# Routing table: one-hots stored with the 16 columns innermost, a written-out count constant, and the dense rows' column left out of the products

## What is computed

```python
y = conv(x, taps)                       # 16 taps along the sequence, per channel
logits = y @ Wr                         # 4096 tokens x 8 experts
w, sel = top_k(logits, 2); w = softmax(w)
gate = sum_k w[k] * one_hot(sel[k], 8)
out = sum_e gate[e] * (y @ We[e] + be[e])
x = x + out
```

## Time and profile before

| | |
|---|---|
| median of three executions | 845.53 us (844.99 to 846.36) |
| the profiled execution | 845.81 us, of which the span of the trace is 844.1 us |
| PE busy | 740.7 us (88%) |
| DVE busy | 564.4 us (67%) |
| ACT busy | 396.8 us (47%) |
| POOL busy | 477.3 us (57%) |
| routing, from the last logits product to the first gather | 537.9 to 577.7 us of the span |

### The profile page before, as it was taken

One profiled execution on the slowest core, in us unless ns is written; L12 is line 12 of the kernel. 1 busy time (PEld: TensorE's weight loads), 2 busy tenths in 40 slices (PEclk: granted clock), 3 DMA queues, 4 the chain that ended last, 5 costly groups with the idle time before them and its releaser, 6 DMA issues.

```text
span 844.1 us, 12610 instructions
## 1 busy us (share of the span) xinstructions
PE 740.7 (88%) x3913; PEld 432.6 (51%) x3945; DVE 564.4 (67%) x831; ACT 396.8 (47%) x635; POOL 477.3 (57%) x738
## 2 busy tenths in 40 slices
PE   1745599999999999999989999657999999899994
PEld 0112244444444444444446653345788888778773
DVE  2469999999999999997734424397834654444442
ACT  2056466666768877776412524034322333333332
POOL 1037889888888888884200000003567766876864
PEclk9987899999999999999999999768999999999998
DMA  9984148899999985555698999986468778877876
GB/s 359 388 328 134 31 88 149 137 182 180 178 180 189 183 157 132 117 116 92 138 232 148 113 116 258 116 197 215 77 126 165 143 136 160 152 146 143 167 143 105
DMA packets 230270, 137.50 MB, mean 163 GB/s; under 512 B 162798, under 2 KB 195054, under 8 KB 229054
## 3 DMA queue, kind: packets, MB, share of 16 engines
q1 hardware_dynamic: 210094, 99.94, 59.0%
q0 software_dynamic: 15456, 36.47, 23.2%
q10 hardware_dynamic: 4656, 0.30, 0.5%
HBM read 80.27 MB, written 35.42 MB: 137 GB/s over the span
## 4 chain that ended last, share of the span: by engine, by line
PE 45%; DMA 13%; POOL 11%; DVE 11%; issue 9%; SPq 6%; ACT 4%; POOLq 0%; DVEq 0%; ACTq 0%
DMA out_x<-YS,IDS 8%; PE PS L1480 8%; PE PS L1452 7%; PE PS L1572 7%; PE PS L1429 7%; PE PS L1441 7%; PE PS L1507 4%; POOL out_x L751 3%; SPq L381 2%; POOL ZR L742 2%; DVE Ih L1085 2%; PE PS L1529 1%; DMA QyT<-Qy 1%; ACT Qh L818 1%; DMA QT<-Qh 1%
## 5 line engine op out<-in xcount | busy, mean ns | idle before, releaser
L1572 PE MATMUL PS<-W,ZH 128*128 x552 | 179.5, 406 | 8.2 <-DVE ZL L1339 6.1
L742 POOL DMA_INDIRECT ZR<-z_scratch,IDG x69 | 69.6, 1008 | 156.1 <-DVE IDS L1303 135.4
L1429 PE MATMUL PS<-W,QyT 128*128 128x512 bf16 x502 | 123.0, 387 | 26.8 <-DMA QyT<-Qy 15.2
L751 POOL DMA_INDIRECT out_x<-YS,IDS x69 | 110.8, 1606 | 59.1 <-SPq L560 29.7
L939 ACT ACTIVATE YS<-YS,SG 128x512 f32<-128x512 f32 x69 | 50.0, 724 | 159.9 <-DVE YS L1357 159.9
L1441 PE MATMUL PS<-W,QyT 128*128 128x512 bf16 x504 | 120.9, 381 | 0.4
L1452 PE MATMUL PS<-W,QT 128*128 128x512 bf16 x498 | 116.4, 383 | 4.4 <-DMA QT<-Qh 2.9
L1572 PEld LDWEIGHTS PS<-W,ZH 128*128 128x128 f32 x552 | 100.4, 191 | 29.7 <-issue 11.5
L1572 PE MATMUL PS<-W,ZL 128*128 x276 | 109.6, 397 | 0.0
L1339 DVE TENSOR_TENSOR ZL<-PS,ZH 128x512 fp32r<-128x512 f32 x69 | 47.7, 691 | 78.2 <-ACT ZH L928 78.2
L1429 PEld LDWEIGHTS PS<-W,QyT 128*128 128x128 bf16 x512 | 49.7, 99 | 90.0 <-DMA QyT<-Qy 17.3
(11 more groups left out here) (217 smaller groups left out, 1059.8 us busy)
## 6 DMA issues: line engine op xcount, KB each, us to landing
XW<-out_x SPq DMA_DIRECT2D x64, 240.0 KB, 4.5
X<-in_x SPq DMA_DIRECT2D x32, 256.0 KB, 10.0
out_x<-X SPq DMA_DIRECT2D x32, 256.0 KB, 3.6
z_scratch<-ZZ SPq DMA_DIRECT2D x8, 1024.0 KB, 24.1
WRAW<-in_We SPq DMA_DIRECT2D x8, 1024.0 KB, 12.6
XR<-in_x SPq DMA_DIRECT2D x20, 256.0 KB, 4.1
stage<-in_w1T SPq DMA_DIRECT2D x4, 1024.0 KB, 8.0
stage<-in_w2T SPq DMA_DIRECT2D x4, 1024.0 KB, 11.9
```

Source lines behind the costliest of these rows:

```text
L742: pool.indirect_dma_start(ZR[m % UZ][:], None, z_d, bass.IndirectOffsetOnAxis(IDG[:, m:m + 1].bitcast(U32), 0)) \
L751: pool.indirect_dma_start(x1_d, bass.IndirectOffsetOnAxis(IDS[:, m:m + 1].bitcast(U32), 0), YS[m % UN][:], None, compute_op=ALU.add).then_ ...
L1429: i = nc.tensor.matmul(GP[:, a, :], QyT[t][:, k, :], W12[:, k, o:o + CH], start=(k == 0), stop=(k == KD - 1))
L1572: x = nc.tensor.matmul(bank[i], zz[i % 2][:, k, :], W2[:, bass.ds(q, 1), part, k, :].rearrange("p o d -> p (o d)"), start=(k == 0 and n == ...
```

## The change

- AOH, BOX and BOH are stored with the 16 columns c innermost: AOH [128, 128, 16], BOX [128, 69, 16], BOH [128, 2, 69, 16]. ScalarE's copies and both operands of TensorE's products now take every 16th element, a step of 32 bytes.
- The constant that the compares read is written out: ION [128, 128, 16], where row m holds 16 times the number m. ScalarE makes it by one copy of 2048 elements from IOSB, after the logits (`lg_done`) because its place was ZZ's. The compares read ION and a row of 16 numbers (`columns`), repeated over m, in place of `over` and `along`.
- VectorE waits for that copy together with the exponentials: `route_e` 2 in place of 1.
- The dense rows' column is left out of the products: laps 0 and 2 have 15 copies and 15 products (`listed`), so that POS needs no marking there: the memset of L1265 is dropped.
- The float copy MTF (L1267) is dropped; SLB is computed from MTI.

```diff
--- before.py
+++ after.py
@@ -190,7 +190,8 @@
         WRAW = [place(f"WRAW{e}", (2 * where(e) + 1) * NEXP, [P, KD, D]) for e in range(E)]
         a = a_T + RING * D
         assert a == 2 * E * NEXP and CC * P <= UN * D and a + UZ * ZW <= a_h
-        AOH = [place(f"AOH{i}", a + CC * P // 2 * i, [P, CC, P], BF16) for i in range(2)]
+        AOH = [place(f"AOH{i}", a + CC * P // 2 * i, [P, P, CC], BF16) for i in range(2)]
+        ION = place("ION", a_h, [P, P, CC], BF16)
         ZR = [place(f"ZR{i}", a + ZW * i, [P, ZW]) for i in range(UZ)]
         YS = [place(f"YS{i}", a_h + D * i, [P, D]) for i in range(UN)]
         ZH = [place(f"ZH{i}", a_h + D * (UN + i), [P, KD, P], F32R) for i in range(2)]
@@ -202,7 +203,7 @@
         PM = place("PM", a + D, [P, OH])
         SEL = place("SEL", a + D + OB, [P, OH * E])
         LGS = [place(f"LGS{g}", a + 2 * D + NCB * g, [P, NCB]) for g in range(NQ)]
-        BOH = [place(f"BOH{i}", a + CC * MT * i, [P, CC, 2, MT], BF16) for i in range(2)]
+        BOH = [place(f"BOH{i}", a + CC * MT * i, [P, 2, MT, CC], BF16) for i in range(2)]
         a += CC * MT * 2
         ZDH, ZDL = (place(n, a + D * i, [P, KD, P], F32R) for i, n in enumerate(("ZDH", "ZDL")))
         a += 2 * D
@@ -237,7 +238,7 @@
         CNT = place("CNT", a, [P, E, NT], BF16)
         TRI, ONB, IOSB = (place(n, a + NR // 2 + P // 2 * i, [P, P], BF16) for i, n in enumerate(("TRI", "ONB", "IOSB")))
         CUM = place("CUM", a_s + 8 * D + NR, [P, E, NT], BF16)
-        BOX = [place(f"BOX{i}", a_T + RING * D + CC * P + CC * MT // 2 * i, [P, CC, MT], BF16) for i in range(2)]
+        BOX = [place(f"BOX{i}", a_T + RING * D + CC * P + CC * MT // 2 * i, [P, MT, CC], BF16) for i in range(2)]
         assert 2 * CC * P // 2 + CC * MT <= UZ * ZW
         a += NR // 2 + 3 * P // 2
         IOS = place("IOS", a, [P, P], I32)
@@ -253,7 +254,7 @@
         a += 8 * E + 8 * UN
         GTS = place("GTS", a, [P, NT, 2])
         a += NT * 2
-        POS, MTF = (place(n, a + NK * i, [P, NK]) for i, n in enumerate(("POS", "MTF")))
+        POS = place("POS", a, [P, NK])
         MTI = place("MTI", a + 2 * NK, [P, NK], I32)
         SLB, MTB = (place(n, a + 3 * NK + NK // 2 * i, [P, NK], BF16) for i, n in enumerate(("SLB", "MTB")))
         a += 4 * NK
@@ -364,13 +365,13 @@
 
             return TORD.index((w, c)) + 1
 
-        def along(t, q, n):
-
-            return t[:, CC * q:CC * q + CC].rearrange("p (c o) -> p c o", o=1).broadcast_to([P, CC, n])
-
-        def over(t, first, n):
-
-            return t[:, first:first + n].rearrange("p (o n) -> p o n", o=1).broadcast_to([P, CC, n])
+        def columns(t, q, n):
+
+            return t[:, CC * q:CC * q + CC].rearrange("p (o c) -> p o c", o=1).broadcast_to([P, n, CC])
+
+        def listed(q):
+
+            return CC if q % 2 else ND
 
 
 
@@ -899,6 +900,9 @@
                 act.wait_ge(x1_out[b], 16 * B)
             act.wait_ge(z_out[0], 16 * NQ)
             nc.scalar.dma_start(ZD[:], bass.AP(z_d.tensor, ND * ZW, [[OB * ZW, P], [SEG, NQ], [1, NI]])).then_inc(zd_in, 16)
+            act.wait_ge(lg_done, 1)
+            act.wait_ge(route_v, 4)
+            nc.scalar.copy(ION[:], IOSB[:].rearrange("p (m o) -> p m o", o=1).broadcast_to([P, P, CC])).then_inc(route_e, 1)
             act.wait_ge(route_v, VM2)
             nc.scalar.activation(EX[:], M2[:], ACT.Exp).then_inc(route_e, 1)
             act.wait_ge(zdt_done, 1)
@@ -913,8 +917,8 @@
                 act.wait_ge(boh_done, 2 * q + 1)
                 if q >= 2:
                     act.wait_ge(tab_done, q - 1)
-                for c in range(CC):
-                    i = nc.scalar.activation(BOH[q % 2][:, c, 0, :], BOX[q % 2][:, c, :], ACT.Copy, scale=float(c + 1 + CC * (q // 2)))
+                for c in range(listed(q)):
+                    i = nc.scalar.activation(BOH[q % 2][:, 0, :, c], BOX[q % 2][:, :, c], ACT.Copy, scale=float(c + 1 + CC * (q // 2)))
                 i.then_inc(num_done, 1)
 
             high(E // 2)
@@ -1241,7 +1245,7 @@
             dve.wait_ge(cnt_done, 1)
             nc.vector.tensor_tensor_scan(CUM[:].rearrange("p e n -> p (e n)"), MROW[:].rearrange("p e n -> p (e n)"),
                                          CNT[:].rearrange("p e n -> p (e n)"), 0.0, ALU.mult, ALU.add).then_inc(cnt_done, 1)
-            dve.wait_ge(route_e, 1)
+            dve.wait_ge(route_e, 2)
             v(nc.vector.tensor_scalar(P1[:], EX[:], 1.0, None, ALU.add))
             v(nc.vector.reciprocal(P1[:], P1[:]))
             v(nc.vector.tensor_tensor(P2[:], P1[:], EX[:], ALU.mult))
@@ -1262,11 +1266,9 @@
                 v(nc.vector.tensor_tensor(CAND[:], oh[:], upto[:], ALU.mult))
                 v(nc.vector.tensor_reduce(POS[:, NT * k:NT * k + NT], CAND[:], AX.X, ALU.add))
 
-            v(nc.vector.memset(POS[:].rearrange("p (k n) -> p k n", k=2)[:, :, ND], -float(P * P)))
             v(nc.vector.tensor_scalar(MTI[:], POS[:], 1.0 / P, 0.5 / P - 0.5, ALU.mult, ALU.add))
-            v(nc.vector.tensor_copy(MTF[:], MTI[:]))
             nc.vector.tensor_copy(MTB[:], MTI[:])
-            v(nc.vector.scalar_tensor_tensor(out=SLB[:], in0=MTF[:], scalar=-float(P), in1=POS[:], op0=ALU.mult, op1=ALU.add))
+            v(nc.vector.scalar_tensor_tensor(out=SLB[:], in0=MTI[:], scalar=-float(P), in1=POS[:], op0=ALU.mult, op1=ALU.add))
 
             dve.wait_ge(zdh_done, 1)
             nc.vector.tensor_tensor(ZDL[:].rearrange("p k m -> p (k m)"), bank[6],
@@ -1277,10 +1279,10 @@
                     dve.wait_ge(tab_done, q - 1)
                     dve.wait_ge(num_done, q - 1)
 
-                nc.vector.tensor_tensor(BOX[h][:], over(IOSB, 0, MT), along(MTB, q, MT), ALU.is_equal).then_inc(boh_done, 1)
+                nc.vector.tensor_tensor(BOX[h][:], ION[:, 0:MT, :], columns(MTB, q, MT), ALU.is_equal).then_inc(boh_done, 1)
                 dve.wait_ge(boh_done, 2 * q + 1)
-                nc.vector.tensor_scalar(BOH[h][:, :, 1, :], BOX[h][:], PIDX[h], None, ALU.mult).then_inc(boh_done, 1)
-                nc.vector.tensor_tensor(AOH[h][:], over(IOSB, 0, P), along(SLB, q, P), ALU.is_equal).then_inc(oh_done, 1)
+                nc.vector.tensor_scalar(BOH[h][:, 1, :, :], BOX[h][:], PIDX[h], None, ALU.mult).then_inc(boh_done, 1)
+                nc.vector.tensor_tensor(AOH[h][:], ION[:], columns(SLB, q, P), ALU.is_equal).then_inc(oh_done, 1)
 
             v(nc.vector.tensor_tensor(GE[:], IOSF[0:1, 0:MT].rearrange("p (m o) -> p m o", o=1).broadcast_to([1, MT, E]),
                                       END[0:1, :].rearrange("p (o e) -> p o e", o=1).broadcast_to([1, MT, E]), ALU.is_ge))
@@ -1542,8 +1544,8 @@
             for q in range(NK // CC):
                 pe.wait_ge(oh_done, q + 1)
                 pe.wait_ge(num_done, q + 1)
-                for c in range(CC):
-                    i = nc.tensor.matmul(bank[7][:, 0:2 * MT], AOH[q % 2][:, c, :], BOH[q % 2][:, c, :, :].rearrange("p v m -> p (v m)"),
+                for c in range(listed(q)):
+                    i = nc.tensor.matmul(bank[7][:, 0:2 * MT], AOH[q % 2][:, :, c], BOH[q % 2][:, :, :, c].rearrange("p v m -> p (v m)"),
                                          start=(q == 0 and c == 0), stop=(q == NK // CC - 1 and c == CC - 1))
                 i.then_inc(tab_done, 1)
                 dense(q)
```

## The result

The changed kernel takes 854.42 us (median of four, 853.78 to 856.70) against 845.26 us for the kernel before: 1.0108 times as long, interval 1.0088 to 1.0128. The forecast of 843.6 us, and the end of the range at 850.0, are wrong. The profiled execution is 853.78 us with a span of 852.0.

A forecast was written before the change was run, and what follows sets the result against it. The prediction took VectorE's chain to L1296 as the bound, with TensorE 0.8 us behind. First product 1.25 us earlier and TensorE's piece cut from 13.96 to 13.79 gave 2.2 us: 845.81 - 2.2 = 843.6 us, range 841.6 to 850.0.

The forecast's parts named there:

- TensorE as the new bound: Routing loop: after the first product TensorE's 13.96 us, cut to 13.79, set the table reader's start; VectorE no longer bounds.
- The step of 32 bytes on TensorE: Products' operands: stepped reads cost nothing over 0.44 ns a column; upper bound 1.14 ns from the convolution's row.
- Rival B: TensorE's products: one-hots read at half rate, 111 ns instead of 61, adding 2.35 us; result 846.0, up to 848.8; chance 0.22.
- ScalarE's copies: Lap copies from BOX to BOH: no extra for the step, 0.157 us each, lap 0's 15 taking 2.36 us.
- CNT's price: ScalarE's copies, other end: 3.3 ns more per element from CNT's stepped write, making a copy 0.385 us; result 852.4.
- rival C: Loop: ScalarE's 62 copies become the bound, reader at 558.2 + 62c (c a copy's time), slower from c = 0.28 us; chance 0.24.
- The compares: VectorE's BOX and AOH: element's share halved (middle value), 1300 to 725 and 2284 to 1217 ns, 6.6 us over four laps.
- The chain to the first product: Before lap 0's products: dropped instructions save 0.33 us, BOX 0.58, one copy fewer; first product 1.25 us earlier.
- The 2.2 us of the forecast: Whole routing stage: table reader L1296 starts at 573.2 instead of 575.41, shortening the kernel by 2.2 us.
- The 0.8 us by which TensorE ended before the reader: End of the loop: TensorE's last product ended at 574.58, L1296 started at 575.41, so TensorE was 0.8 us behind the bound.
- rival E: TensorE's clock in the loop rises later after the earlier start, costing 1.3 us at most; result 844.9; chance 0.09.
- From the first gather on: Expert stage: gathers come 2.2 us earlier without collisions, and the rest of the span stays 266.4 us.

The follow-up runs named there:

- e16: Changed kernel with AOH, BOX and BOH in groups of 2 columns innermost instead of 16: 1.0000 of the kernel before's time (0.9977 to 1.0023).
- e13: Changed kernel with all three tiles in groups of 2 columns innermost, on another chip than e16: 0.9995 of the kernel before's time (0.9974 to 1.0016).
- e9: Changed kernel with all three tiles in groups of 2 columns and the dense products of laps 2 and 3 after the last table products: 0.9977 (0.9959 to 0.9996).
- e11: The kernel before, unchanged, traced a second time on another chip: 846.4 us in its group, table's reader 36.7 us after the logits' copies.
- e8: Changed kernel with AOH and BOX in groups of 4, BOH in the old layout, laps 2 and 3's dense products moved last: 0.9982 (0.9952 to 1.0012).
- e6: Changed kernel with all three tiles in groups of 2 columns innermost, dense products not moved: one run, 859.77 us against 859.20 for the kernel before.
- e7: Changed kernel with AOH and BOX in the old layout with old compares, BOH alone columns innermost: one run, 867.15 us against 859.20 before.
- e5: Changed kernel with BOH alone back in the old layout: 1.0006 of the kernel before's time (0.9973 to 1.0039).

## Why the prediction was wrong

**TensorE as the new bound: right.** The step "from there TensorE is the bound" holds, and VectorE waits for it as foreseen (2.46 us before the reader in e16). It is why a price on TensorE comes through in full.

**The step of 32 bytes on TensorE: the failed step.** I put its price at nothing, with 1.14 ns a column from the convolution as the upper bound. Measured were 1.78 ns a column, 245 ns a product in place of 61. In sum: lap 0 with 3.61 us in place of 1.77, laps 1 and 3 with 3.92 in place of 0.97, lap 2 with 3.64 in place of 0.97, 10.4 us; and `dense` of laps 0 to 2 with 9.95 in place of 9.09. From T0 to the recorded end of the last product (584.92) that is 25.4 us against the forecast's 13.8. Rival B was the mechanism, and its price was wrong: "half its rate" instead of a quarter. The bound of 1.14 ns came from a misread row. The kernel has 256 matmuls of the convolution (2 halves, 8 groups, 8 numbers, 2 parts), and the trace has 512 records of them:

```profile
L1480 PE MATMUL PS<-XW,BD x512: 440/477/487, 419.1 to 500.7; 128*64 128x128 f32 x171
```

So the 146 ns are the time of a record, of which each f32 product has two, and a product of 128 columns takes some 290 ns at a granted clock of 1.00, 2.27 ns a column: above the 1.78, and no upper bound of 1.14. The records start in pairs, 24 ns apart, with 265 ns to the next pair (medians), which speaks for two of them running side by side, one for each half of the output's partitions. No run tested that, nor what part of the 2.27 ns is the step. The Trainium skill (SBUF — State Buffer, Specifications) had the rule that I set aside: lines of 16 bytes, at least two hits for full bandwidth. The runs agree with the lines and differ on the number: two bf16 columns in 16 bytes take 121 ns a product, twice the contiguous 61; four are needed (63).

**ScalarE's copies: priced wrong too.** I took the MEMSET's side, 157 ns; measured were 311, two thirds of the way from there to CNT's price of 385. By rival C's own formula the reader would be at 558.2 + 62 x 0.311 = 577.5, 2.1 us late. That it never decided is TensorE's doing: lap 0's copies delay T0, and from then on they are done before they are needed. Beside the forecast, T0 came 2.0 us late (23.4 us after LGS, forecast 21.4) and the stretch from T0 on took 11.6 us more, together the 13.7 by which the reader missed its forecast; the copies are the small part. The 8-element MEMSET of VectorE was no measure for ScalarE's copies of 69 elements; why it shows no price itself, no run tested.

**The compares: right.** 724 to 735 and 1217 to 1220 ns, against 725 and 1217. The middle value was the right choice, and so was the sentence that VectorE's 6.6 us are not the stage's gain.

**The chain to the first product:** 0.33 us, and BOX's 0.58, came; 15 copies took 4.67 us in place of 2.36.

**The 2.2 us of the forecast** were seen in no run, even without the step. The kernel with products at 63 ns took 0.9995 and 1.0000 of the time before (e13 and e16); 2.2 us would be 0.9974, at the edge of the first interval and just outside the second. But GTS's issue held ScalarE in both, and no run has this kernel where it doesn't. What the traces show is which terms were smaller. The chain's part came in e9: the first product started 1.1 us earlier after LGS than in e11. The 0.8 us by which TensorE ended before the reader of the table belong to that one trace. In e11, where lap 0's `dense` took 4.13 us, the last product ends at 577.02, only 0.1 us before the reader:

```profile
575.86 1.16 PE L1546 MATMUL PS<-BOH,AOH 128*128 128x138 bf16 x16
```

```profile
577.13 0.23 DVE L1296 TENSOR_SCALAR KSL<-PS 128x69 f32<-128x69 f32 x1
```

And the clock took part of the rest: rival E priced the later rise at 1.3 us, and the 4.12 to 4.64 us of lap 0's `dense` in e16, e11 and e9 are 0.8 to 1.3 more than the 3.34 that I took from one trace. I had taken the one trace that I had for the rule.

**From the first gather on:** one for one where the transfers don't bind (264.7 and 266.2 us after it in the two traces of the changed kernel, 266.5 and 267.1 before). Elsewhere the first rows land late, and an earlier list mostly waits (e8 beside e6).

## What to carry to other kernels

Before storing a tile with a step to speed up its writer, price every reader, the one with the most elements per nanosecond first: the compares of the four laps won 6.6 us on VectorE, and 62 products lost 10.4 us on TensorE. Keep at least four two-byte elements of the moving operand that follow each other in the same 16 bytes; groups of 2 columns innermost gave the compares their full rate and cost TensorE 2 ns a product. Before a row of the trace bounds a price, count its records against the calls in the kernel, and look whether two of them run side by side.

## What was unexpected

- TensorE's price per 16 bytes doesn't follow its clock: 241 ns a product at a granted clock of 0.50, 245 at 1.00. Only the moving operand pays it in full; stepped weights lengthen their load from 98 to 148 ns and the product by 4.
- The stepped write costs ScalarE 2.2 ns an element ((311 - 157) / 69), the stepped read half of that, and both together no more than the write. VectorE's stepped write is the dearest: 1104 elements took 2650 ns in e7, against 507 contiguous and 1226 with a stepped read in e5.
- The same kernel is 1.6% slower on some chips (859.2 against 845.3 us). The traces from there differ in the routing stage: the issue of GTS's two transfers takes 9.2 to 10.7 us of ScalarE instead of 1.6 to 2.7.
